# The third and seventh small products trade places, two x blocks trade numbers, and VectorE's order behind them is rewritten

## The reference

```python
x = x + einsum('bct,bcd->bdt', x, W0[itok_B_0_15])       # mixes the 64 rows of a batch
x = x + einsum('bct,bcd->bdt', x, W1[itok_B_0_15])
x = x + x @ W.T + 0.5 * (x @ A[itok_B_0_2]) @ lora_b.T   # 1024 x 1024, rank 32 addition
x = x + x @ W3[itok_B_3_7].T                             # 1024 x 1024, one of 8 matrices per batch
```

## Time and profile before

| what | us |
|---|---|
| median of three runs | 388.74 |
| all three | 390.9, 388.74, 388.54 |
| the profiled execution, its time | 388.97 |
| the profiled execution, its span | 387.1 |

### The profile page before, as it was taken

The page is one execution under the profiler, slowest core; times in us unless marked ns, Lnnn a source line. Parts: engine busy times, 40 slices in busy tenths (PEclk is TensorE's granted clock), DMA queues, the critical chain, the costliest instruction groups (busy, mean ns, idle before and its releaser), DMA issues.

```text
span 387.1 us, 7697 instructions
## 1 busy us (share of the span) xinstructions
PE 375.1 (97%) x1726; PEld 310.2 (80%) x1727; DVE 281.9 (73%) x328; ACT 228.3 (59%) x306; POOL 120.6 (31%) x161
## 2 busy tenths in 40 slices
PE   8999999999999859999999999999999999999995
PEld 5888888888888748888888888888888888888784
DVE  3796998699897975618669459775498645999753
ACT  3688577675369337224647366934578536779443
POOL 0000230201020000005567437564176631676600
PEclk9999999999999998999999999999999999999999
DMA  7975806735978515133446315662247522565223
GB/s 254 426 269 212 333 0 255 288 108 195 211 183 284 108 73 186 68 109 121 168 151 188 99 48 155 212 211 58 56 149 224 178 58 57 190 199 161 59 62 86
DMA packets 17419, 62.43 MB, mean 161 GB/s; under 512 B 1922, under 2 KB 2114, under 8 KB 14914
## 3 DMA queue, kind: packets, MB, share of 16 engines
q1 hardware_dynamic: 16304, 56.96, 43.9%
q0 software_dynamic: 576, 4.19, 5.8%
q10 hardware_dynamic: 466, 0.44, 0.3%
HBM read 52.15 MB, written 8.39 MB: 156 GB/s over the span
## 4 chain that ended last, share of the span: by engine, by line
PE 92%; DVE 4%; issue 1%; DMA 1%; ACT 1%; ACTq 0%; DVEq 0%
PE ps L1720 44%; PE ps L1571 10%; PE ps L1572 10%; PE ps L1573 10%; PE ps L1746 4%; PE ps L1598 3%; PE ps L1639 3%; PE ps L1612 2%; PE ps L1812 2%; PE ps L1552 2%; PE ps L1553 2%; PE ps L1554 2%; DMA eye<-eye_c 1%; DVE ring L1029 1%; DVE xT L1118 1%
## 5 line engine op out<-in xcount | busy, mean ns | idle before, releaser
L1720 PE MATMUL ps<-ring,aT 128*128 x752 | 173.3, 389 | 0.0
L1720 PEld LDWEIGHTS ps<-ring,aT 128*128 128x128 f32 x752 | 141.0, 188 | 29.6 <-issue 0.5
L543 POOL TENSOR_TENSOR aT<-xT,aT 128x512 fp32r<-128x512 f32 (+1 forms) x36 | 55.4, 1558 | 45.5 <-ACT aT L882 40.5
L1571 PE MATMUL ps<-ring 128*128 128x512 f32 x176 | 69.1, 393 | 0.0
L1572 PE MATMUL ps<-ring 128*128 128x512 f32 x176 | 69.0, 392 | 0.0
L1573 PE MATMUL ps<-ring 128*128 128x512 f32 x176 | 68.8, 391 | 0.0
L1442 DVE TENSOR_TENSOR ring<-raw,ring 128x1024 f32 (+1 forms) x40 | 63.6, 1650 | 5.9 <-ACT ring L868 5.9
L888 ACT ACTIVATE aT<-ps 64x1024 fp32r<-64x1024 f32 x32 | 32.7, 1022 | 48.8 <-PE ps L1720 48.4
L1470 DVE TENSOR_TENSOR stage<-ps,stage 64x1024 f32<-64x1024 f32 x30 | 36.7, 1222 | 27.5 <-ACT stage L897 26.8
L1459 DVE TENSOR_TENSOR aT<-ps,aT 64x1024 fp32r<-64x1024 f32 x32 | 39.1, 1223 | 21.5 <-ACT aT L888 20.9
L897 ACT ACTIVATE stage<-ps 64x1024 f32<-64x1024 f32 x30 | 30.5, 1017 | 24.0 <-PE ps L1746 23.6
(11 more groups left out here) (133 smaller groups left out, 413.2 us busy)
## 6 DMA issues: line engine op xcount, KB each, us to landing
raw<-w3t SPq DMA_DIRECT2D x40, 512.0 KB, 4.5
out<-stage SPq DMA_DIRECT2D x30, 256.0 KB, 3.1
ring_f<-xt SPq DMA_DIRECT2D x6, 1024.0 KB, 7.6
xT<-xt SPq DMA_DIRECT2D x6, 1024.0 KB, 8.4
raw<-xt SPq DMA_DIRECT2D x5, 1024.0 KB, 6.9
ring_f<-wt SPq DMA_DIRECT2D x3, 1024.0 KB, 7.4
xT<-wt SPq DMA_DIRECT2D x2, 1024.0 KB, 17.6
raw<-xt POOLq DMA_DIRECT2D x2, 1024.0 KB, 9.4
```

The costliest lines, as they stand in the source:

```text
L543: pool.tensor_tensor(x3_split(i, ks, P + h * T, T), xT[:, ks, bass.ds(which[h] * T, T)], as_f32(x3_split(i, ks, h * T, T)), ALU.subtract). ...
L1571: pe.matmul(dst, hi_of(qw)[:, k, cs], hi_of(qx)[:, k, :], start=start and k == 0, stop=False, skip_group_check=True)
L1720: last = pe.matmul(acc(i)[:, n, :], x3_split(i, k, start, P), ring[:, bass.ds(off + (part * D + n * 512), 512)], start=(k == 0 and j == 0) ...
```

## The change

In TensorE's order L7 stands ahead of L3. The x blocks that were 9 and 10 swap numbers: the block that is made first (the lower half, loaded to the spare place `raw_of(1)`) is now 9 and sits in slot 3, the one made second (the upper half) is 10 and sits in slot 4. The functions that use them, the tables of last uses and of the events waited for follow. The load of the new block 10 waits, as before, for L3, which now ends one small product later.

On VectorE the two blocks stand together; R21 follows them; then w 5, R12, and the low-rank parts of chunk 2 come ahead of the plan's pieces. Of the plan, `take(2)` stands ahead of c22(0) and the rest behind x block 11. VectorE now waits for `x_lo` before it writes the low part of w 5, as that lies where block 9's raw data was. On ScalarE x block 11 stands ahead of the eight copies `select(12..15)`.

```diff
-    x_slot = lambda n: (3, 4, 5, 3, 4, 5, 3, 4, 5, 4, 3, 4, 5, 3)[n]
+    x_slot = lambda n: (3, 4, 5, 3, 4, 5, 3, 4, 5, 3, 4, 4, 5, 3)[n]
...
-    LEAF = (("L1", "A11", "B11"), ("L5", "S1", "T1"), ("L2", "A12", "B21"), ("L6", "S2", "T2"), ("L3", "S4", "B22"),
-            ("L7", "S3", "T3"), ("L4", "A22", "T4"))
+    LEAF = (("L1", "A11", "B11"), ("L5", "S1", "T1"), ("L2", "A12", "B21"), ("L6", "S2", "T2"), ("L7", "S3", "T3"),
+            ("L3", "S4", "B22"), ("L4", "A22", "T4"))
...
-    x_before = lambda n: {8: ("L5", 0, 1), 9: ("L3", 0, 1), 10: ("L7", 0, 1), 11: x_last[9], 12: x_last[8],
-                          13: x_last[10]}.get(n) or x_last[n - 3]
+    x_before = lambda n: {8: ("L5", 0, 1), 9: ("L7", 0, 1), 10: ("L3", 0, 1), 11: x_last[10], 12: x_last[8],
+                          13: x_last[9]}.get(n) or x_last[n - 3]
...
-            sp.dma_start(x10_raw, x_block(2, 2)).then_inc(s("x_in10"), 16)
-            load_x(9, 1, 2)
+            sp.dma_start(x9_raw, x_block(2, 2)).then_inc(s("x_in9"), 16)
+            load_x(10, 1, 2)
...
-            x_from(10, x10_raw, "x_in10", 16)
-            x_loaded(9)
+            x_from(9, x9_raw, "x_in9", 16)
+            x_loaded(10)
             wait_l2(act, ("L4", 0, 1))
             w_from(5, kw, "S4", 16)
             low_out(2)
+            x_from(11, stg, "T1", 32)
             for pair in range(12, 16):
                 select(pair)
-            x_from(11, stg, "T1", 32)
...
-            x_los(10, x10_raw)
+            x_los(9, x9_raw)
+            x_los(10)
             leaf_add("L4", ps_y, v21, r21, "R21")
-            x_los(9)
+            dve.wait_ge(s("x_lo"), HALF * 10)
+            w_los(5, kw)
             leaf_add("L3", ps_z, r12, r12, "R12", ("V12", 1))
-            take()
-            w_los(5, kw)
             low_parts(2)
+            take(2)
             c22(0)
             x_los(11, stg)
+            take()
             x_los(12)
             c12(0)
             x_los(13, kw)
...
-            leaf(4, ps_z, False, lambda o: (s("R22"), o + 1), (leaf_b, 0, 1))
-            leaf(5, ps_y, False, lambda o: (s("U2"), o + 1))
+            leaf(4, ps_y, False, lambda o: (s("U2"), o + 1))
+            leaf(5, ps_z, False, lambda o: (s("R22"), o + 1), (leaf_b, 0, 1))
...
-                        low_rank(2 + j, 9 + 3 * j, 10 + 3 * j)
+                        low_rank(2 + j, 10 + 2 * j, 9 + 4 * j)
...
-                    last = main(5, 10 + 3 * j, ps_l2(2, j, o), o, False, False)
+                    last = main(5, 9 + 4 * j, ps_l2(2, j, o), o, False, False)
```

More of the change, by code:

```diff
@@ L158, in build @@
     t4_of = lambda j: out_block(2, j)
-    x10_raw = raw_of(1)
+    x9_raw = raw_of(1)
     a22 = raw_of(0)
@@ L255, in build @@
     x_last = [("low", 0, 3), ("low", 1, 3), ("C11", 0, 3), ("C11", 1, 3), ("P6", 0, 3), ("P7", 0, 3), ("P6", 1, 3), ("P7", 1, 3),
-              ("C22", 0, 1), ("low", 2, 3), ("C12", 0, 3), ("C22", 1, 1), ("low", 3, 3), ("C12", 1, 3)]
-    x_before = lambda n: {8: ("L5", 0, 1), 9: ("L3", 0, 1), 10: ("L7", 0, 1), 11: x_last[9], 12: x_last[8],
-                          13: x_last[10]}.get(n) or x_last[n - 3]
+              ("C22", 0, 1), ("C12", 0, 3), ("low", 2, 3), ("C22", 1, 1), ("low", 3, 3), ("C12", 1, 3)]
+    x_before = lambda n: {8: ("L5", 0, 1), 9: ("L7", 0, 1), 10: ("L3", 0, 1), 11: x_last[10], 12: x_last[8],
+                          13: x_last[9]}.get(n) or x_last[n - 3]
     w_last = [("P1", 1, 3), ("C11", 1, 3), ("P6", 1, 3), ("P7", 1, 3), ("C22", 1, 1), ("C12", 1, 3)]
```

## The result

| kernel | median of its runs, us | lowest to highest | profiled execution, us | its span |
|---|---|---|---|---|
| before | 388.87 | 388.54 to 390.9 | 388.97 | 387.1 |
| changed | 382.81 | 382.52 to 382.9 | 382.79 | 380.9 |

The changed kernel takes 0.9827 of the time of the kernel before (95% interval 0.98 to 0.9855). It is 6.1 us faster, where 7.3 was forecast; the forecast time was 381.7, and 382.8 was measured.

The account below looks back on a forecast made before the run. TensorE, busy 375.1 of 387.1 us, was taken to bound the kernel, so gains come only through its waits. The terms 1.4 + 4.7 + 1.42 - 0.2 = 7.3 us, from 388.97, gave 381.7; range 380.9 to 384.2.

Parts of the forecast that it names:

- Term 1: Small products: L7 directly after L6 needs U2, whose copies have 0.5 us slack, so no gain or loss: 0.
- Term 2: Start of chunk 2's low-rank projection: block 10 lands 4.8 us after issue, TensorE starts at 130.7, not 132.14: gain 1.4.
- the bound that the prediction kept: Block 10's landing: 4.8 us or less gains at most 1.6; 6.9 gives -0.7; 11.0 gives -4.8.
- Term 3: First low-rank correction: its wait goes, 7.93 us after the projection's start instead of 12.63, slack 0.3: gain 4.70.
- the template of j = 1: Same program piece at j = 1, no plan in the way: correction 7.93 us after projection, C12 10.20 after.
- Term 4: Correction to C12: without the long wait the ten matmuls run at full clock, 2.27 us instead of 3.69: gain 1.42.
- Term 5: C12's first tile: two plan pieces ahead of c22 make TensorE wait anew, 0.2 us: term -0.2.
- What was put at nothing: Block 11's T1 load (issued 129.3, landing 8.0 later), the plan's later rest, block 13, adapter loads, `select` copies: no cost.
- the late landing: Rival: block 10 lands in 6.9 us, projection starts at 132.8, gain 5.2, time 383.8; chance 0.13.
- the clock's fall: Rival: small waits on the low-rank chain add up, the clock falls, 1.42 not refunded: 383.1; chance 0.07.
- the second projection's wait: Rival: at j = 1 the plan's rest delays VectorE, TensorE waits 2.0, or 3.4 with clock fall: 385.1; chance 0.05.
- the slower side: Rival: block 10's load takes 11.0 us, projection starts at 136.9 and the clock falls: 389.1; chance 0.02.

Follow-up runs that it names:

- the first experiment: The changed kernel with the order of the small products undone (L3 ahead of L7), all else kept: 381.83 us, ratio to before 0.9819.

## Why the prediction was right, and where its sum was off

The main mechanism was right: the plan stood ahead of a chain that TensorE needed. Both the run with that edit alone (383.08) and the run with that edit undone (389.8) show it. The sum was 1.1 us too high. Term by term, from the two profiled executions:

| term | forecast gain | measured | from |
|---|---|---|---|
| 1, small products | 0 | -0.64 | L7 at 116.67; L6's last matmul 115.80 + 0.23 |
| 2, projection's wait | 1.4 | 1.22 | 1.60 to 0.38 |
| 3, low-rank wait | 4.70 | 4.59 | 12.63 to 8.04 |
| 4, clock | 1.42 | 1.39 | 3.69 to 2.30 |
| 5, wait at C12 | -0.2 | 0 | C12 follows the correction by 2.30, at j = 1 by 2.27 |

The measured terms sum to 6.56. The profiled executions differ by 388.97 - 382.79 = 6.18; the rest, 0.4, was lost ahead of the changed place, in the first products, and comes and goes between executions.

- **Term 1 failed** in the profiled execution. The step read "Slack is 0.5 at either tile", from one execution. That slack lies behind ScalarE's earlier work, which hangs on VectorE's low part of T2, and that on where POOL's addition falls. In the changed kernel's profile they met, 1.17 us were lost on VectorE (2.39 against 1.22), and they used up the 0.5 and 0.64 more. The prediction had said that U2's cover was gone and priced it at the 0.6 of one copy; it should have asked what else could make U2 late. With L3 in between the same lateness costs nothing (the first experiment). It is not a fixed cost either: of the eight profiles in which L7 follows L6 directly, L7 waited for U2 in this one alone, and not in the second profile of the same kernel.
- **Term 2** was right in its mechanism and close in size: R21 is what TensorE waits for, and the load landed in 4.7. Its issue was at 122.91, 1.16 behind the forecast, and all but 0.1 of that is term 1's 0.64 and the 0.4 from ahead. In the second profile of the changed kernel the wait was 0.86, with 5.3 us from the issue to ScalarE's start. Other executions show the bound that the prediction kept: 6.1 and 6.3 us from issue to ScalarE's start in two, with waits of 1.58 and 1.84.
- **Term 3 and the template of j = 1** held within 0.1. The thin slack of 0.3 on the chain was not used up.
- **Term 4** held, and the runs now bracket it: no fall with waits of 1.47, 1.60, 1.84 and 1.92, a fall with 3.46, 3.60, 4.45 and 5.17.
- **Term 5** was 0.2 too gloomy: c22's first tile came just in time.
- **What was put at nothing** stayed at nothing for TensorE: no wait at the second projection (it starts at 159.58 without one), and none in the adapter stage, though the plan is ready 10 us later. One step behind it was off: T1 of block 11 was issued by POOL at 131.94, not 129.3, and landed 9.0 later; ScalarE, which was free 1.49 us before, took block 11 up at 141.04, just behind that. TensorE did not feel it.
- **Of the rivals**, the late landing is real and occurs in single executions; the clock's fall, the second projection's wait and the slower side did not come. The slower side's mechanism, the later load, showed in the kernel before with the products alone swapped: 0.5% slower. In the changed kernel its effect is the 0.4 that is left of the projection's wait, and 1.58 to 1.84 in an execution with a late landing.
- **Not foreseen at all** was that the swap, one of the change's parts, makes it slower, and that undoing it gives a better kernel. The prediction priced the later load within term 2 but never set the version without it beside it: there the load would have landed behind other work of ScalarE, and the whole 1.60 was to be had.

## What to carry to other kernels

Work that nobody waits for yet belongs behind the chain that the bounding engine needs, cut so that no single block delays the next link: the same 6.5 us made TensorE wait nowhere in two parts, and cost 5.7 us in one part ahead of c22. When a step loses the work that covered it, look one engine farther back for what can make it late, and at more than one execution. Test each part of a bundle alone; here one reordering brought nearly all, and another took some back.

## What the runs showed of the hardware that was not expected

Waits of TensorE of up to 1.92 us left the clock at its upper level, and those of 3.46 us or more drew the lower one; no wait between the two was seen. How much longer the work behind it took depends on what that work was: 1.4 us behind the wait of 4.45, and 2.6 us in the projection behind the wait of 3.46 (6.62 us against 4.06). Only the first of these reached the end time; the second was taken up by the next wait, which the plan had set.

A VectorE operation that was held up beside POOL's addition shows it as a longer record (2.39 us and not 1.22) and not as idle time, so a list of waits does not show it.

The same 1 MB load, with nothing changed around it, was taken up by ScalarE 4.75 to 4.9 us after its issue in five profiles of kernels that wait for it, 5.3 in one, and 6.1 and 6.3 in two. Why was not tested.
